# State-space sums in two PSUM banks in turn, and the gated recurrence's products and sums as scans over pairs

## What is computed

```python
def step(h, inp):                       # state-space stage, 256 channels d x 128 states s, 128 steps t
    u_t, dt_t, B_t, C_t = inp
    dA = jnp.exp(dt_t[:, :, None] * A_mean)
    dB = dt_t[:, :, None] * B_t[:, None, :]
    h = dA * h + dB * u_t[:, :, None]
    y_t = jnp.einsum('bds,bs->bd', h, C_t)          # the state-space sum
    return (h, y_t)

def step(h, x_t):                       # gated recurrence, 128 steps t, h is 16 x 128
    fused = jax.nn.sigmoid(jnp.concatenate([x_t, h], axis=-1) @ w_W + w_b)
    hidden_state, output_state = jnp.split(fused, 2, axis=-1)        # r, z
    memory_state = x_t @ wx_W + wx_b + hidden_state * (h @ wh_W + wh_b)
    h_new = output_state * h + (1.0 - output_state) * jnp.tanh(memory_state)
    return (h_new, h_new)
```

## Time and profile before

| | |
|---|---|
| median of 3 runs | 6887.28 us (6886.77 to 6894.01) |
| the profiled execution's own time | 6891.72 us |
| its span, first to last instruction | 6889.9 us |
| mean granted clock of TensorE | 0.965 |
| state-space scan, first scan to last copy of sums | 4040.3 to 5711.6 us |
| gated recurrence, its 128 steps | 5765.5 to 6052.2 us |

### The profile page before, as it was taken

One profiled execution on the slowest core, in us unless ns is written; L12 is line 12 of the kernel. 1 busy time (PEld: TensorE's weight loads), 2 busy tenths in 40 slices (PEclk: granted clock), 3 DMA queues, 4 the chain that ended last, 5 costly groups with the idle time before them and its releaser, 6 DMA issues. The chain is left out here.

```text
span 6889.9 us, 153257 instructions
## 1 busy us (share of the span) xinstructions
PE 5728.5 (83%) x49639; PEld 3103.4 (45%) x49913; DVE 5672.1 (82%) x11657; ACT 4672.8 (68%) x10329; POOL 2701.3 (39%) x2035
## 2 busy tenths in 40 slices
PE   5888888888888888888888858888888888953999
PEld 3555555555555555555555413333333334532543
DVE  4899998998989989989899689999999995456333
ACT  6898998998989989989899744444444443333332
POOL 3222222222222222222222169999999991000000
PEclk9999999999999999999999979999999999976999
DMA  0000000000000000000000010000000001000000
GB/s 8 2 2 2 2 2 2 2 2 2 2 2 2 2 2 2 2 2 2 2 2 2 11 40 4 3 4 4 3 4 3 4 3 34 0 0 0 0 0 6
DMA packets 14204, 30.55 MB, mean 4 GB/s; under 512 B 3666, under 2 KB 11603, under 8 KB 12435
## 3 DMA queue, kind: packets, MB, share of 16 engines
q1 hardware_dynamic: 13586, 22.47, 1.2%
HBM read 15.12 MB, written 7.34 MB: 3 GB/s over the span
## 5 line engine op out<-in xcount | busy, mean ns | idle before, releaser
L425 ACT ACTIVATE rx_junk<-rx_z 128x384 bf16<-128x384 f32 x2178 | 1369.6, 631 | 0.3
L1089 POOL TENSOR_TENSOR hc<-hh,cg 128x512 f32<-128x512 f32 x1024 | 1278.2, 1269 | 79.7 <-DVE hh L1069 75.3
L1010 ACT ACTIVATE ps_m<-ps_m,aneg 128x508 f32<-128x508 f32 x1024 | 673.9, 659 | 875.6 <-DVE hh L1069 833.1
L1069 DVE TENSOR_TENSOR_SCAN hh<-ps_m,bx 128x512 f32<-128x512 f32 x1024 | 1214.4, 1209 | 13.8 <-POOL bx L1093 13.8
L519 POOL TENSOR_TENSOR rx_z<-rx_z 128x512 f32<-128x512 f32 x256 | 386.6, 1510 | 1791.0 <-DVE rx_z L617 1791.0
L974 PE MATMUL ps_m<-hc,pick 128*128 128x512 f32 x2048 | 1055.7, 599 | 9.8 <-POOL hc L1089 8.5
L657 DVE TENSOR_REDUCE rh_ends<-rh_z 128x4 f32<-128x1536 f32 (+1 forms) x512 | 846.5, 1695 | 125.4 <-ACT rh_z L443 125.4
L525 POOL TENSOR_TENSOR rx_z<-rx_z 128x1024 f32<-128x1024 f32 x274 | 656.6, 2396 | 73.4 <-DVE rx_z L620 36.7
L316 PE MATMUL r_ps<-rh_z,negid 128*128 128x256 f32 x2048 | 500.1, 386 | 110.8 <-ACT r_ps L437 109.1
L344 PE MATMUL r_ps<-rx_z,negid 128*128 128x512 f32 x1096 | 506.0, 604 | 58.8 <-POOL rx_z L525 58.8
L340 PE MATMUL r_ps<-rx_z,negid 128*128 128x256 f32 x2192 | 528.4, 384 | 30.9 <-DVE rx_z L620 11.8
(11 more groups left out here) (395 smaller groups left out, 10947.3 us busy)
## 6 DMA issues: line engine op xcount, KB each, us to landing
rows_scratch<-pc SPq DMA_DIRECT2D x48, 128.0 KB
rows<-rows_scratch SPq DMA_DIRECT2D x128, 48.0 KB
ew<-in_e SPq DMA_DIRECT2D x3, 1024.0 KB, 9.1
rh_z<-in_x_dn SPq DMA_DIRECT2D x1, 1024.0 KB, 4.7
xcur<-in_x_dn SPq DMA_DIRECT2D x1, 1024.0 KB, 5.3
out_x<-xcur SPq DMA_DIRECT2D x1, 1024.0 KB, 3.9
qi<-in_f_q SPq DMA_DIRECT2D x1, 384.0 KB, 3.3
xpw<-in_xp_t SPq DMA_DIRECT2D x1, 257.0 KB
```

The costliest lines, as they stand in the source:

```text
L425: e.activation(junk[:, n % JUNK], xz[i][:, :, n, 2:K2].rearrange("p c k -> p k c"), ACT.Copy, accum_out=xsum[:, i, n:n + 1]).then_inc(x_fo ...
L1010: e.activation(da[un % NDA][:, :, 1:T], ps[:, un % 2, :].rearrange("p (n t) -> p n t", n=NG4)[:, :, 1:T], ACT.Exp, scale=aneg[:, 0:1]).the ...
L1069: e.tensor_tensor_scan(hh[un % NBUF][:], da[un % NDA].rearrange("p n t -> p (n t)"), bx[un % NBUF][:], 0.0, ALU.mult, ALU.add).then_inc(sc ...
L1089: e.tensor_tensor(hc[un % NHC][:], hh[un % NBUF][:], cg[:], ALU.mult).then_inc(weighted, 1)
```

## The change

*State-space sums.* The two halves of a group now use banks 6 and 7 in turn. The first sum of a half starts its bank afresh, so the product of zeros and its two tiles go. The last six sums of a half are issued behind the rows of the first six units of the next half (`late`). ACT copies a finished bank after the first iteration of the next half; PE waits for the copy two halves back (`moved`, at unit 6). The first half's late sums find zeros: DVE clears six `hc` buffers and bank 7 at the start; the memset of the second row buffer moves behind the start values, and SP waits for each buffer by itself inside its loop. At the end of all come the last six sums and one copy.

*Gated recurrence.* Pairs of elements replace three tiles. `cand_in` holds (r, part from x) for each step and column; bank `at+2` holds (0, candidate + bias), seeded with `hbias` and with the product added to each second column; one scan gives a*0 + r = r, then candidate*r + part from x. `keep` holds (0, 1-z), `blend` (tanh, h*z); a second scan gives h_new into `state`, which PE reads directly. DVE then seeds the gates and the bias of step t+2, waits for its scan, and copies h to `gh`. The loop has five idle products for six.

```diff
-        yh = sb("yh", [128, G, H2, NG4 * T])
+        ysum = sb("ysum", [128, 1 + G * H2, NG4 * T])
+        yh = ysum[:, 1:, :].rearrange("p (g h) x -> p g h x", g=G)
...
-            zero = ss("zero", [128, 128])
-            blank = ss("blank", [128, W4])
...
+            NSET = LAG + 1 + NDA + 4
...
-                    for b in range(2):
-                        e.wait_ge(cleared[b], 2)
                     with e.Fori(0, G * NI) as it:
                         for b in range(2):
+                            e.wait_ge(cleared[b], 2)
                             e.wait_ge(dt_bc, it * UP + (b + 1) * CH)
...
-                    def state_sum(un, gh):
-                        e.wait_ge(weighted, gh * HU + un + 1 + NBUF)
-                        e.matmul(ps[:, 6, :], pick[:, 128 - un:256 - un], hc[un % NHC][:], start=False, stop=True,
+                    def state_sum(half, un, base):
+                        e.wait_ge(weighted, base + un + 1 + NBUF + NHC)
+                        e.matmul(ps[:, 6 + half, :], pick[:, 128 - un:256 - un], hc[un % NHC][:], start=(un == 0), stop=True,
                                  skip_group_check=True).then_inc(summed, 1)
-                    with e.Fori(0, G * H2) as gh:
-                        e.wait_ge(moved, gh + 1)
-                        e.matmul(ps[:, 6, :], zero[:], blank[:], start=True, stop=True, skip_group_check=True)
-                        for un in range(HU):
...
-                            e.matmul(ps[:, 2 + un % 2, :], ones3[:], rows[1][b][:, j, :], start=True, stop=True).then_inc(w_bc, 1)
-                            e.wait_ge(decay, gh * HU + un + 1)
-                            e.matmul(ps[:, un % 2, :], ones3[:], rows[0][b][:, j, :], start=True, stop=True).then_inc(dt_bc, 1)
-                            if un >= LAG:
-                                state_sum(un - LAG, gh)
-                        for un in range(HU - LAG, HU):
-                            state_sum(un, gh)
+                    with e.Fori(0, G) as g:
+                        for half in range(H2):
+                            done = g * (H2 * HU) + half * HU
+                            for un in range(HU):
...
+                                e.matmul(ps[:, 2 + un % 2, :], ones3[:], rows[1][b][:, j, :], start=True, stop=True).then_inc(w_bc, 1)
+                                e.wait_ge(decay, done + un + 1)
+                                e.matmul(ps[:, un % 2, :], ones3[:], rows[0][b][:, j, :], start=True, stop=True).then_inc(dt_bc, 1)
+                                if un == LAG:
+                                    e.wait_ge(moved, g * H2 + half + 1)
+                                if un >= LAG:
+                                    state_sum(half, un - LAG, done)
+                                else:
+                                    late = HU + un - LAG
+                                    e.wait_ge(weighted, done + un - LAG + 1 + NBUF + NHC)
+                                    e.matmul(ps[:, 7 - half, :], pick[:, 128 - late:256 - late], hc[late % NHC][:], start=False,
+                                             stop=True, skip_group_check=True).then_inc(summed, 1)
+                    for un in range(HU - LAG, HU):
+                        state_sum(1, un, (G * H2 - 1) * HU)
...
-                        e.wait_ge(summed, gh * 128 + 128 + NHC)
...
+                    def units(it):
...
+                    with e.Fori(0, G) as g:
+                        for half in range(H2):
+                            units(g * NI + half * (NI // H2))
+                            e.wait_ge(summed, g * (H2 * HU) + half * HU + NHC)
+                            e.activation(ysum[:, half:half + 1 + (G - 1) * H2, :][:, bass.ds(g * H2, 1), :].rearrange("p a x -> p (a x)"),
+                                         ps[:, 7 - half, :], ACT.Copy).then_inc(moved, 1)
+                            with e.Fori(1, NI // H2) as i:
+                                units(g * NI + half * (NI // H2) + i)
+                    e.wait_ge(summed, G * H2 * HU + NHC)
+                    e.activation(ysum[:, G * H2, :], ps[:, 7, :], ACT.Copy).then_inc(moved, 1)
...
-                    for b in range(2):
-                        e.memset(rows[0][b][:], 0.0).then_inc(cleared[b], 1)
+                    e.memset(rows[0][0][:], 0.0).then_inc(cleared[0], 1)
+                    for i in range(LAG):
+                        e.memset(hc[(HU - LAG + i) % NHC][:], 0.0).then_inc(grp, 1)
+                    e.memset(ps[:, 7, :], 0.0).then_inc(grp, 1)
...
-                    e.memset(zero[:], 0.0).then_inc(grp, 1)
-                    e.memset(blank[:], 0.0).then_inc(grp, 1)
...
-                    e.memset(bx[0][:, 3:4], 0.0).then_inc(summed, NHC)
+                    e.memset(bx[0][:, 3:4], 0.0).then_inc(summed, NHC - LAG)
...
+                    e.memset(rows[0][1][:], 0.0).then_inc(cleared[1], 1)
...
-WARM = 6
+GRU_WARM = 5
+LSTM_WARM = 6
...
-        gx = sb("gx", [128, 3, COLS + N])
+        gx = sb("gx", [128, 2, COLS + 2 * N])
+        cand_in = sb("gcand_in", [128, T, N, 2])
+        upd = sb("upd", [128, N]); keep = sb("gkeep", [128, N, 2]); blend = sb("gblend", [128, N, 2])
+        cand = sb("gcand", [128, N, 2]); state = sb("gstate", [128, N, 2]); hbias = sb("ghbias", [128, N, 2])
...
-        V0 = 2
+        V0 = 4
...
-                e.wait_ge(warm, 2)
+                e.wait_ge(warm, 9)
...
-                        e.wait_ge(vec, t * KV + V0)
-                        h = gh[:, bass.ds(t, 1), :].rearrange("p a n -> p (a n)")
+                        e.wait_ge(vec, t * KV + V0 - 3)
+                        h = state[:, :, 1]
                         e.matmul(ps[:, at, 0:N], gw[:, 1, 0:D], h, start=False, stop=True, skip_group_check=True).then_inc(prod, 1)
-                        e.matmul(ps[:, at + 2, 0:N], gwh[:], h, start=True, stop=True).then_inc(prod, 1)
+                        e.matmul(ps[:, at + 2, 0:2 * N].rearrange("p (n two) -> p n two", two=2)[:, :, 1], gwh[:], h,
+                                 start=False, stop=True, skip_group_check=True).then_inc(prod, 1)
                         e.matmul(ps[:, at + 1, 0:N], gw[:, 1, D:2 * D], h, start=False, stop=True, skip_group_check=True).then_inc(prod, 1)
-                        for _ in range(WARM):
+                        for _ in range(GRU_WARM):
...
+                    to = gx[:, k // 4, c * 512:(c + 1) * 512] if k < 8 else \
+                        cand_in[:, c * 32:(c + 1) * 32, :, 1].rearrange("p t n -> p (t n)")
+                    e.activation(to, ps[:, k % 8, :], ACT.Identity, bias=gb[:, k // 4:k // 4 + 1]).then_inc(moved, 1)
...
-                        e.activation(reset[:], ps[:, at, 0:N], ACT.Sigmoid).then_inc(act, 1)
+                        e.activation(cand_in[:, bass.ds(t, 1), :, 0].rearrange("p a n -> p (a n)"), ps[:, at, 0:N], ACT.Sigmoid).then_inc(act, 1)
...
-                        e.activation(new[:], ps[:, at + 1, 0:N], ACT.Sigmoid, scale=-1.0).then_inc(act, 1)
-                        e.wait_ge(vec, t * KV + V0 + 2)
-                        e.activation(th[:], r2[:], ACT.Tanh).then_inc(act, 1)
+                        e.activation(keep[:, :, 1], ps[:, at + 1, 0:N], ACT.Sigmoid, scale=-1.0).then_inc(act, 1)
+                        e.wait_ge(vec, t * KV + V0 + 1)
+                        e.activation(blend[:, :, 0], cand[:, :, 1], ACT.Tanh).then_inc(act, 1)
...
+                e.memset(keep[:], 0.0).then_inc(warm, 1)
+                e.memset(hbias[:], 0.0).then_inc(warm, 1)
+                e.wait_ge(warm, 4)
+                e.wait_ge(loaded, 80)
+                e.tensor_copy(hbias[:, :, 1], gb[:, 3:4].to_broadcast([128, N])).then_inc(warm, 1)
+                e.tensor_copy(state[:, :, 1], gh[:, 0, :]).then_inc(warm, 1)
+                e.wait_ge(warm, 6)
...
-                e.memset(r1[:], 0.0).then_inc(vec, 1)
...
-                def seed(t, at):
-                    e.tensor_copy(ps[:, at:at + 2, 0:N], gxt[:, 0:2, bass.ds(t, 1), :].rearrange("p q a n -> p q (a n)")).then_inc(vec, 1)
-                seed(0, 0)
+                def seed_gates(t, at):
+                    e.tensor_copy(ps[:, at:at + 2, 0:N], gx[:].rearrange("p q (t n) -> p q t n", n=N)[:, :, bass.ds(t, 1), :]
+                                  .rearrange("p q a n -> p q (a n)"))\
+                        .then_inc(vec, 1)
+                def seed_bias(at, done):
+                    e.tensor_copy(ps[:, at + 2, 0:2 * N], flat(hbias[:])).then_inc(done, 1)
+                for at in (0, 3):
+                    seed_gates(at // 3, at)
+                    seed_bias(at, warm)
+                e.memset(upd[:], 0.0).then_inc(vec, 2)
+                e.wait_ge(vec, V0)
+                e.memset(cand[:], 0.0).then_inc(warm, 1)
                 with e.Fori(0, T // STEPS) as block:
                     for step in range(STEPS):
                         t = STEPS * block + step
                         at = 3 * (step % 2)
```

(19 more changed lines are left out.)

## The result

| | before | after |
|---|---|---|
| median (20 runs each) | 6887.41 us | 6960.15 us |
| lowest to highest | 6883.08 to 6894.01 | 6886.81 to 6989.42 |
| profiled execution, its span | 6891.72, 6889.9 | 6890.35, 6888.5 |
| first to last scan of the state-space stage | 1665.8 us | 1634.1 us |
| first to last weight load of the 128 gated steps | 284.6 us | 318.7 us |

The changed kernel takes 1.0068 times as long by the means of the runs (1.0106 by the medians), 95% interval of the first 1.0039 to 1.0096: slower, by less than 2%, where 6791 us was forecast. Its times stand in three groups, nine runs at 6887 to 6896, eight at 6959 to 6969 and three at 6981 to 6989; the profiled execution belongs to the first.

The account below looks back on a forecast made before the run. DVE was taken to pace the state-space scan, with stalls at changes of half, and a step-by-step chain the recurrence. From 6891.7, -43.4 and -53 gave 6795, scaled to 6791 us; range 6780 to 6822.

Parts of the forecast that it names:

- Change of half: State-space scan: seven changes of half lose 7.0 us each through the order of PE's queue; removing them wins 49.0 us.
- Rival 2: State-space scan: the change of half only moves its stall, POOL lagging and PE stopping at late sums; 6834 us, chance 0.06.
- The first iteration's 1.4 us: Start of the state-space scan: 51.95 against 50.55 us, put down to filling the empty pipeline.
- Change of group: State-space scan, three changes: DVE waits for its last scan and copies B uncovered; +1.9 us each, +5.6 in all.
- The step: Gated recurrence: one step falls from 2.22 to 1.78 us (chain 1.76 to 1.85), 56 us over 128 steps.
- floor of PE: Gated recurrence: PE is free 1.77 us after the load with five idle products, 1.99 with six; no step is shorter.
- Rival 1: Gated recurrence: the product written to each second PSUM element is slow; step 2.00 us, time 6819 us, chance 0.13.
- The turn of the loop: Gated recurrence, where ACT loads its tables: r due 0.12 us earlier, 7 x 0.12 and some slack lost, +1.5 us.
- Rival 3: Gated recurrence: TensorE falls to half clock, step 3.5 us, time 7010 us, slower than before; chance 0.03.

Follow-up runs that it names:

- before_gap2: Kernel before, plus an unread ScalarE activation of 1800 columns ahead of r in the first step of each turn: 6906.4 us, ratio 1.0027.
- groups_pe: `act_written_out` with PE's loop over the four groups of the state-space scan written out too: 6786.9 us, ratio 0.9852.
- table_first: Changed kernel plus a one-element sigmoid, waiting for nothing, at the head of each ScalarE turn of the recurrence: 6799.0 us, ratio 0.9871.
- idle_at_turn: Changed kernel with ten idle products for five in the first step of each turn, table load left late: 6804.8 us, ratio 0.9887.
- six_idle: Changed kernel with six idle products in each step for five: 6818.1 us, ratio 0.9900.
- act_written_out: Changed kernel with ScalarE's loop of the recurrence written out, so its table loads once: 6791.3 us, ratio 0.9868.

## Why the prediction was wrong

**Change of half: right.** Every change of half inside a group takes 50.65 us like any iteration, none of the 7.0 us is left, ScalarE's copy costs nothing, and PE doesn't wait for POOL there. Rival 2 is out. The 7.0 us were more than the order of a queue: 5.9 to 6.0 at the change itself, and 0.6 to 1.7 in the iteration behind it, in which the clock fell; in `before_gap2` it stayed up behind the first two changes of half, and there the next iteration took 50.56. The first iteration's 1.4 us, which I put down to the filling of the pipeline, had the clock at 0.50 up to 4049.67, too; after, with the clock up from 4031.63, that iteration takes 50.65. An iteration takes 0.09 more than before (31 x 0.09 = 2.8 us), with DVE's wait for POOL's product at 0.52 for 0.43; I had no term for that, and no run looked for its cause.

**Change of group: a term mis-sized.** Forecast +1.9 each; measured +6.6, +5.0 and +4.7 over an iteration of 50.65. The copy of B is +1.8, as `groups_pe` shows: that step was right to 0.1. What I left out is that PE's loop now turns here over a body of 256 units for 128. The Trainium skill ("Runtime: NRT & Kernel Launch", Instruction fetch mechanics) says that a taken branch to a place outside the window that the engine holds has to fetch it first. The same section of the Trainium skill gives PE room for 2048 instructions. The trace has 1285 records of PE's queue from one branch to the next before and 2578 after, one number under that and one over it, and the branch went from 0.21 to 3.3 us and more, so it agrees, as far as records stand for instructions; what is fetched no run here shows. The second pause comes with the branch, and so does most of the half clock (in `groups_pe` it is left behind one change of group in three); what each of them adds is not separated. In all the stage gave 31.7 us for 43.4; without the 10.7 us that this term was short it would have been 42.4.

**The step: right, for a partly wrong reason.** 1.76 us against 1.78 forecast (1.76 to 1.85 by the chain), scans of 0.22 and 0.23 us. But 1.77 was no floor of PE: its next weights load while the last idle product runs, so with five the step can be 1.66, and with six it is 1.88 (0.58 + 6 x 0.216) where I had 1.99. It was the chain that set 1.76.

**Rival 1 is out.** The strided product takes 0.37 to 0.38 us for its two passes, as before, and in both kernels the next product starts 0.22 us after it has started. The Trainium skill ("PSUM — Partial Sum Buffer", Specifications) led to that rival; for 16 columns in every second place the trace shows no cost.

**The turn of the loop: the step that failed.** I forecast +1.5 us for all turns, on the ground that the table load runs ahead as in the earlier trace rows and r is due only 0.12 us earlier. But r is now written to an address that depends on t. In the trace a register instruction of L1269 now works out that address ahead of the operation and carries the wait for the product (5758.04 at this turn), and the table load follows it (5758.11). Before, only the count of this wait depended on t, the sigmoid itself carried the wait, and the load stood ahead of it (5837.09). So the load now starts when the product is there, and 1.27 us come at each of eight turns: 10 us. `table_first` shows that the place of the load decides: the same load, ahead of the wait, and the turn costs 0.60.

**Rival 3, at 0.03, is what happened.** Its mechanism (half clock, PE as the bound) and its price were near: a step of 3.5 forecast, 3.23 measured. Its chance was wrong, because I argued from the mean, that PE is busier than before. Over the loop it is; at a turn it pauses for 1.09 us where before it was 0.40, and I had that place in hand and priced it at 0.12. The times follow from it: 6803 us with the clock up (6890.35 less 62 x 1.47, plus 3 x 1.27 for turns that cost nothing at half clock; `idle_at_turn` measured 6804.8), and from there 1.47 us for every step behind the fall. Behind the fifth load 62 steps are left: 6890. Behind the second 110, 162 - 8: 6957. Behind the first 126, 185 - 9: 6979. These are the three groups of times, to within 12 us. That the two slower groups fell there is worked out, not seen: the only profile of the changed kernel is of the first.

From the forecast to the fast case: 6791, +12 in the state-space stage, +9 at the turns, -3 in the steps, 6809 (6805 measured in `idle_at_turn`, which would have been in the range, 1.1% faster than before). The fall costs 87 to 176 us more.

**Open.** Which of the eight turns brings the clock down differs from run to run, and no run shows why. Nor is it known whether the sixth idle product or the shorter pause kept the clock in `six_idle`, nor, with five, where between 0.42 and 1.09 us the fall begins.

## What to carry to other kernels

An operation that gets its address from a loop counter can have its wait carried ahead of what the compiler sets in front of it (a counted wait with a fixed address did not, before): look where a table load of ScalarE stands against that wait before costing it as hidden. Where a loop is filled with idle products to hold TensorE's clock, look at the longest pause in a turn, too, and not only at the mean: here one pause of 1.09 us cost the clock for the rest of the loop, and filling it or moving what caused it kept the clock. Doubling the body of a loop can have a price at its turn: 0.2 us became 3.3 to 3.8 here (up to 5.05 in `act_written_out`), with a second pause of 1.8 to 2.8 soon behind it.

## What the hardware showed that I had not expected

- TensorE fell to 1.2 GHz in a loop in which it was busy for 114.53 of 120 us, after single pauses of 1.09 us. It then stayed there to the end of the loop, in the window shown for 196 us, while its rows show no break; 16 products of 512 columns in a row, 6.9 us with the step's own five, brought it back.
- With six idle products for five the same recurrence kept 2.4 GHz over pauses of 0.88 us, and the old one over pauses of 1.04. In the state-space stage it held over a pause of 1.25 us at each change of iteration.
- PE's branch over a body of 2578 recorded instructions takes 3.3 to 3.8 us in the changed kernel and 3.5 to 5.05 in `act_written_out`, over 1285 it takes 0.21 to 0.23, and behind the long one PE stops a second time, for 1.8 to 2.8 us in the changed kernel.
- PE loads the weights of the next matmul while the last idle product runs: at 5802.77, 0.11 us ahead of the first product that uses them.
- Written out on all three engines, with constant addresses and waits, the step went from 1.75 to 1.66 us with the same operations in it.
